# Two-layer graph convolution with a mixture-of-experts block on one core: layer 2 reduces its gathered rows in pairs

## The chip, the cores and the metric

One core of a Trainium2 chip runs the whole program. The metric is the device time of one execution in microseconds; the median of three runs of the kernel before is 1064.74 us.

## The reference

```python
x, src, dst: 1250 nodes of 512 floats, 41250 edges sorted by dst (each node has a loop to itself)

def graph_conv_max(x, src, dst, W_rel, b, W_root):
    agg = segment_max(x[src], dst, num_segments=1250)      # maximum over a node's neighbours
    agg = where(isfinite(agg), agg, 0.0)
    return agg @ W_rel.T + b + x @ W_root.T

h = relu(graph_conv_max(layernorm(x), ..., W1_rel, b1, W1_root))   # layer 1
h = relu(graph_conv_max(h, ..., W2_rel, b2, W2_root))              # layer 2
x = x + h
# then 8 experts, each takes the 512 rows with the highest softmax-over-rows score of its logit:
out_e = gelu(layernorm(x)[idx] @ W1 + b1) @ W2 + b2;  x = x + scatter_add(vals * out_e)
```

## The kernel before, in words

The nodes are sorted by their number of neighbours and cut into ten tiles of 128 (`NQ`), the lightest first. A tile with n neighbours at most needs n rounds: round r fetches for each of the 128 nodes the row of its r-th neighbour (128 rows of 2 KB, out of a table in HBM) and takes the maximum with what is there. Tile 0 has only 98 nodes; its other 30 partitions take over what the heaviest nodes have beyond the limit of the last tile. The last tile passes its maxima through `carry`.

Four parties work on the rounds, and meet only through semaphores:

- GpSimd (POOL) issues one indirect DMA per row of rounds into a ring of 12 slots (`SLOTS`, L884), two to a group (`GROUP`, function `gathers`, L873). Before each group it waits for `done` (the slots are free), for `here` (at most six rows, `FLYING`, under way) and for `s_ic[h]` (the group's two index columns are in `ic`).
- SyncE (SP, function `landed`, L840) waits for each row's landing on `s_gather[j]` and increments `ready` per row (L845), `here` per group (L846), and then loads the group's next two index columns with a DMA of its own (L820, one per group).
- VectorE (DVE) reduces. In layer 1 `pool_pair` (L944) takes two slots in one operation of 128x1024 (L951). In layer 2 `one_round` (L998) takes one slot in an operation of 128x512 (L1004), into the two halves of `acc` in turn; `vec_tile` (L1047) starts a tile with two operations that fill the halves from `carry` (L1057, L1058) and ends it with L1074 to L1080.
- TensorE (PE) and ScalarE (ACT) turn the tile's maxima into the layer's output. In layer 2 PE runs the feed-forward block of tile q (`ffn`, L1178) and in the midst of it the aggregate's product of tile q+1 (`neighbours`, L1146; transposes at L1130, product at L1159), which waits for `fin`, the end of DVE's tile q+1. DVE in turn has done ten rounds of its next tile (`AHEAD`) when it waits for that product (L1026, `add_and_moments`), two more (`PEELED`), and then normalizes (L1044, `normalize`), which lets PE begin the next `ffn`.

In layer 1 PE also makes the first 20 neighbours of every node by one-hot products (L1243), so that layer 1 has 186 gathers and layer 2 338. The counts of rounds are worked out on the device (L664 to L712): layer 1's are rounded up to even for every tile (L665 to L668), layer 2's only in total, by giving the last tile one more round where the sum is odd (L709 to L712).

Of the kernel before, what the change touches and what calls it, by code (L numbers as in the profile page):

```python
# [7 lines left out]
P = 128  # L8
N, E, D = 1250, 41250, 512
# [4 lines left out]
NQ = -(-N // P)  # L14
# [5 lines left out]
SLOTS = 12  # L20
MAXR = 64
UNROLL = 4
FLYING = 6
AHEAD = 10
PEELED = 3 * UNROLL
MINR = PEELED + UNROLL + 1
# [5 lines left out]
GROUP = 2  # L32
SUBS = SLOTS // GROUP
# [43 lines left out]
def build(nc, x, src, dst, w1_rel, b1, w1_root, w2_rel, b2, w2_root, wr, fw1, fb1, fw2, fb2, out):  # L77
    with ExitStack() as ctx:
# [9 lines left out]
        def dram(name, shape, dt=F32):  # L88
# [114 lines left out]
        both1 = sb("both1", [1, NQ], I32)  # L203
        evens, nvalid, base = sb("evens", [NQ, 1], I32), sb("nvalid", [P, NQ]), sb("base", [P, NC])
# [6 lines left out]
        ic = sb("ic", [P, SLOTS], I32)  # L211
# [32 lines left out]
            neg bits bias pairs pa ga merge here""".split()  # L244
        S = {n: sem("s_" + n) for n in names}
        s_gather = [sem(f"s_gather{j}") for j in range(SLOTS)]
        s_ic = [sem(f"s_ic{h}") for h in range(SUBS)]
# [416 lines left out]
        cv.do(v.tensor_scalar(nmax[:, 0:1], nmax[:, 0:1], float(MINR), None, ALU.max))  # L664
        cv.link(v.tensor_scalar(nmax[:, 1:2], nmax[:, 1:2], float(MINP), 1.0, ALU.max, ALU.add))  # L665
        cv.link(v.tensor_copy(evens[:, :], nmax[:, 1:2]))
        cv.link(v.tensor_scalar(evens[:, :], evens[:, :], -2, None, ALU.bitwise_and))
        n_nmax = cv.link(v.tensor_copy(nmax[:, 1:2], evens[:, :]))  # L668
# [38 lines left out]
        cv.do(v.tensor_copy(meta[:, 0:NQ], pl[0:1, 0:NQ]))  # L707
        cv.do(v.tensor_scalar(meta[:, NQ + 1:2 * NQ], pl[0:1, NQ + 1:2 * NQ], -1.0, None, ALU.add))
        cv.link(v.tensor_scalar(meta[:, NQ:NQ + 1], pl[0:1, NQ:NQ + 1], float(GROUP - 1), None, ALU.add))  # L709
        cv.link(v.tensor_scalar(meta[:, NQ:NQ + 1], meta[:, NQ:NQ + 1], -GROUP, None, ALU.bitwise_and))  # L710
        cv.link(v.tensor_tensor(meta[:, 2 * NQ:2 * NQ + 1], meta[:, NQ:NQ + 1], meta[:, NQ - 1:NQ], ALU.subtract))
        n_meta = cv.link(v.tensor_scalar(meta[:, 2 * NQ:2 * NQ + 1], meta[:, 2 * NQ:2 * NQ + 1], -1.0, None, ALU.add))  # L712
# [32 lines left out]
        starts = [a.value_load(meta[0:1, q:q + 1], min_val=0, max_val=(NQ - 1) * MAXR) for q in range(NQ)]  # L745
# [24 lines left out]
        v.sem_inc(S["done"], SLOTS)  # L770
        g.sem_inc(S["here"], FLYING)
        a.wait_ge(S["xs"], 16 * NQ)
        for l in range(2):
# [38 lines left out]
            if l == 0:  # L812
                c = s.value_load(meta1[0:1, NQ:NQ + 1], min_val=NQ * MINP // 2, max_val=NQ * LCAP // 2)
            else:
                c1, c = c, s.value_load(meta[0:1, NQ:NQ + 1], min_val=NQ * MINR, max_val=NQ * MAXR + GROUP) // GROUP
            lists_l = (idx1, idxf)[l]

            def load_indices(i, h):

                s.dma_start(ic[:, h * GROUP:(h + 1) * GROUP], lists_l[:, bass.ds((i * SUBS + h) * GROUP, GROUP)])\  # L820
                    .then_inc(s_ic[h], 16)

            after(s, ca, n_idxf if l else n_idx1s[0])
            for h in range(SUBS):
                if l:
                    s.wait_ge(s_ic[h], ((c1 + (SUBS - 1 - h)) // SUBS + 1) * 16)
                load_indices(0, h)
# [21 lines left out]
            with s.Fori(0, c // SUBS) as i:  # L849
                for h in range(SUBS):  # L850
                    landed(i, h)
            for h in range(SUBS - 1):
                with s.If(c % SUBS > h):
                    landed(c // SUBS, h)
# [767 lines left out]
```

## Time and profile before

| what | value |
|---|---|
| median of 3 runs (lowest, highest) | 1064.74 us (1062.21, 1070.73) |
| profiled execution, span from first to last instruction | 1161.8 us |
| mean granted TensorE clock in it | 0.860 |
| busy: PE, DVE, POOL, ACT | 791.1, 715.0, 627.7, 269.3 us |

For the profiled execution no time of its own is given beside its span, so the span stands for it; it is 97.1 us above the median of the runs, which were made without a profile. Times of rows below are microseconds from the start of the span. A row of a timeline has start, duration, engine, line, operation, and in brackets how long the engine sat idle before it and what released it; "issue" means nothing that the profile shows, "remote" something outside the core's engines. SPq is the sequencer of SP.

### The profile page before, as it was taken

Reading aid. Unit: us, or ns where it says so; the run is one execution under the profiler, and the core shown is the slowest. Engines: PE = TensorE matmul, PEld = TensorE weight load, DVE = VectorE, ACT = ScalarE, POOL = GpSimd, SP = SyncE. Lnnn points to the kernel's source line nnn. Section 1 sums busy time; section 2 is a strip of 40 time slices with the busy share of each in tenths; the row PEclk is TensorE's granted clock in tenths of the full one; section 3 lists DMA queues with packets and bytes.
Section 4 is the critical chain, followed back from the end, with each engine's and each line's share of the span. In section 5 each row is a group of like instructions: output and inputs, shape, how many; then the busy total and the mean of one; then the engine's idle time right before and its main releaser. Section 6 shows DMA issues by size and latency. Waiting matters only on the chain.

```text
span 1161.8 us, 12528 instructions
## 1 busy us (share of the span) xinstructions
PE 791.1 (68%) x2358; PEld 362.5 (31%) x2358; DVE 715.0 (62%) x1428; ACT 269.3 (23%) x436; POOL 627.7 (54%) x627
## 2 busy tenths in 40 slices
PE   0256148888778787550287777869756959777988
PEld 0133013334333333220143333334322424333443
DVE  4769557777666857624565454536543646555888
ACT  0283412333211230010012212122211112212432
POOL 6550363555556656736666645665665476662012
PEclk9778569999998898795688989979887979889989
DMA  5730664666666656586667757765767577776497
GB/s 136 267 104 2 236 184 136 189 189 195 197 189 182 195 175 178 169 288 175 176 175 262 231 164 230 222 209 179 243 211 224 163 233 211 226 213 188 161 380 290
DMA packets 114789, 231.67 MB, mean 199 GB/s; under 512 B 53596, under 2 KB 58080, under 8 KB 111255
## 3 DMA queue, kind: packets, MB, share of 16 engines
q0 software_dynamic: 46304, 149.99, 42.8%
q1 hardware_dynamic: 54346, 38.56, 11.1%
q10 hardware_dynamic: 14092, 42.57, 9.8%
q8 instruction: 19, 0.31, 0.1%
q14 instruction: 28, 0.23, 0.1%
HBM read 196.18 MB, written 37.49 MB: 201 GB/s over the span
## 4 chain that ended last, share of the span: by engine, by line
PE 27%; issue 23%; DVE 22%; another core or an unknown queue 8%; DMA 7%; SPq 5%; ACT 4%; POOL 2%; DVEq 1%; ACTq 1%; POOLq 0%; PEld 0%
PE pp L1194 6%; PE prow L1159 5%; DMA mem<-tab,ic 5%; PE pp L1243 5%; PE pp L1212 5%; DVE mem L1589 2%; DVE acc L940 2%; DVE weights L951 2%; SPq L820 2%; DVE mem L1441 1%; SPq L845 1%; PE pl L1174 1%; POOL mem L884 1%; DVE mem L608 1%
## 5 line engine op out<-in xcount | busy, mean ns | idle before, releaser
L884 POOL DMA_INDIRECT mem<-tab,ic x524 | 546.9, 1044 | 362.3 <-issue 214.8
L1004 DVE TENSOR_TENSOR acc<-acc,mem 128x512 f32<-128x512 f32 x338 | 222.9, 694 | 174.3 <-issue 89.0
L940 DVE TENSOR_TENSOR acc<-acc,pp 128x1024 f32<-128x1024 f32 x90 | 109.7, 1219 | 88.7 <-PE pp L1243 41.5
L1212 PE MATMUL pp<-weights,mem 128*128 128x512 f32 x320 | 152.1, 624 | 14.8 <-issue 12.3
L1194 PE MATMUL pp<-weights,xnT 128*128 128x512 f32 x320 | 152.9, 622 | 0.0
L1243 PE MATMUL pp<-weights,LT 128*128 128x512 bf16 x300 | 81.9, 421 | 62.6 <-DVE acc L940 21.5
L1159 PE MATMUL prow<-weights,aggT 128*128 128x512 f32 x152 | 91.2, 745 | 43.3 <-ACT aggT L1350 33.9
L951 DVE TENSOR_TENSOR weights<-weights,mem 128x1024 f32<-128x1024 f32 x83 | 101.5, 1222 | 9.9 <-DVE weights L951 4.2
L1243 PE MATMUL pp<-weights,slots 128*128 128x512 bf16 x300 | 75.2, 394 | 32.4 <-DVE acc L940 21.7
L1212 PEld LDWEIGHTS pp<-weights,mem 128*128 128x128 f32 x320 | 62.9, 201 | 93.2 <-issue 90.5
L1383 ACT ACTIVATE mem<-pp 128x512 f32<-128x512 f32 x80 | 46.9, 597 | 159.1 <-PE pp L1212 85.1
L1194 PEld LDWEIGHTS pp<-weights,xnT 128*128 128x128 f32 x320 | 59.4, 196 | 70.1 <-issue 70.1
L1243 PEld LDWEIGHTS pp<-weights,LT 128*128 128x128 bf16 x300 | 30.3, 105 | 115.9 <-issue 42.0
L1159 PEld LDWEIGHTS prow<-weights,aggT 128*128 128x128 f32 x152 | 36.2, 245 | 83.7 <-issue 44.2
L1243 PEld LDWEIGHTS pp<-weights,slots 128*128 128x128 bf16 x300 | 29.3, 100 | 79.9 <-DVE acc L940 25.5
L1130 PE MATMUL prow<-ident,agg 128*128 128x128 f32 x80 | 15.2, 322 | 53.9 <-DVE agg L1080 50.4
L1026 DVE TENSOR_TENSOR hst<-prow,mem 128x512 f32<-128x512 f32 x10 | 6.9, 690 | 70.2 <-PE prow L1159 45.4
L1174 PE MATMUL pl<-weights,xnT 128*128 128x512 f32 x80 | 44.1, 681 | 0.0
L1144 PE MATMUL prow<-weights,rootT 128*128 128x512 f32 x80 | 38.6, 605 | 0.0
L1599 POOL DMA_INDIRECT out<-x2t,nodei x1 | 1.3, 1262 | 64.3 <-DVE x2t L1594 64.3
L1375 ACT ACTIVATE mem<-prow 128x512 f32<-128x512 f32 x40 | 23.9, 598 | 46.3 <-remote 36.1
L1575 PE MATMUL pp<-weights,mem 128*128 128x512 f32 x72 | 32.4, 593 | 1.1 <-issue 1.1
(342 smaller groups left out, 888.2 us busy)
## 6 DMA issues: line engine op xcount, KB each, us to landing
yd<-mem ACTq DMA_DIRECT2D x18, 1024.0 KB
weights<-yd SPq DMA_DIRECT2D x9, 2048.0 KB, 13.2
mem<-tab,ic POOLq DMA_INDIRECT x524
weights<-in_L_ffn_W SPq DMA_DIRECT2D x9, 512.0 KB
weights<-in_L_ffn_W ACTq DMA_DIRECT2D x7, 512.0 KB
LT<-ttd ACTq DMA_DIRECT2D x5, 640.0 KB
slots<-ttd ACTq DMA_DIRECT2D x5, 640.0 KB
ic<-idxf SPq DMA_DIRECT2D x175, 1.0 KB
```

The costliest lines, as they stand in the source:

```text
L884: g.indirect_dma_start(rings[l][:, j, :], None, table, bass.IndirectOffsetOnAxis(ic[:, j:j + 1], 0)).then_inc(s_gather[j], 16)
L940: v.tensor_tensor(acc[:, :, :], acc[:, :, :], pp[j % 2][:, :, :], ALU.max).then_inc(S["pa"], 1)
L951: v.tensor_tensor(accg, accg, pair, ALU.max).then_inc(S["done"], 2)
L1004: v.tensor_tensor(acc[:, side, :], acc[:, side, :], rings[l][:, bass.ds(r % SLOTS, 1), :].rearrange("p a d -> p (a d)"), ALU.max).then_inc ...
L1144: t.matmul(pg, rootT[:, c, :], wroot[0][:, c, :], start=False, stop=False)
L1159: ins = t.matmul(pg, aggT[:, c, :], wrel[l][:, c, :], start=l == 1 and c == 0, stop=c == C - 1)
L1174: ins = t.matmul(pl[:, :], xnT[:, c, :], wroot[1][:, c, :], start=False, stop=c == C - 1)
L1194: ins = t.matmul(ph[w % 2].rearrange("p (e f) -> p e f", e=2), xnT[:, c, :], w1s[:, 2 * w:2 * w + 2, c, :], start=False, stop=c == C - 1)
L1212: ins = t.matmul(po[e % 2][:, :], hT[:, e * FC + f, :], w2s[:, e, f, :], start=f == 0, stop=f == FC - 1)
L1243: ins = t.matmul(pp[j % 2][:, k, :], sel[u][:, j * KP + k, :], hot[:, j, w, :], start=w == 0, stop=w == 2)
L1383: a.activation(ystage[:, e, :], po[e % 2][:, :], ACT.Copy).then_inc(S["oe"], 1)
L1575: t.matmul(po[u][:, :], dg[:, u, e, :], expert(q, e), start=e == 0, stop=False)
```

## The change

Layer 2 uses layer 1's pair operation, and both layers count in pairs: each of the 12 pairs of two laps of the ring (`LAP`) has a semaphore that both of its gathers increment, per layer; SP waits once per pair and increments `ready` once; `here` is gone and POOL waits for `ready`. SP loads twelve index columns at a time, after every sixth pair, into one half of an `ic` of 24 columns, and POOL waits for them once per six pairs. Layer 2's count of every tile is rounded up to even. A tile of layer 2 starts with the operation that fills `acc` from `carry` and takes the first pair at once (the first form in `pool_pair`), so that L1057, L1058 and their wait go. The count of rounds before DVE waits for the product stays ten (five pairs), and of those before it normalizes twelve.

```diff
-UNROLL = 4
-FLYING = 6
-AHEAD = 10
-PEELED = 3 * UNROLL
-MINR = PEELED + UNROLL + 1
+FLYING = 3
+AHEAD = 5
+PEELED = 6
+MINR = 2 * (PEELED + 1)
...
+PAIR = 2
+SUBS = SLOTS // PAIR
+LAP = 2 * SUBS
...
-        ic = sb("ic", [P, SLOTS], I32)
+        ic = sb("ic", [P, 2 * SLOTS], I32)
...
-        cv.do(v.tensor_scalar(nmax[:, 0:1], nmax[:, 0:1], float(MINR), None, ALU.max))
+        cv.do(v.tensor_scalar(nmax[:, 0:1], nmax[:, 0:1], float(MINR), 1.0, ALU.max, ALU.add))
...
-        cv.do(v.tensor_copy(meta[:, 0:NQ], pl[0:1, 0:NQ]))
...
+        cv.link(v.tensor_scalar(meta[:, :], pl[0:1, 0:2 * NQ + 1], 0.5, None, ALU.mult))
+        n_meta = cv.link(v.scalar_tensor_tensor(both2[:, :], meta[:, 0:NQ], 64.0, meta[:, NQ + 1:], ALU.mult, ALU.add))
...
-            def landed(i, h):
-
-                before = (c1 + (SUBS - 1 - h)) // SUBS if l else 0
-                for j in range(h * GROUP, (h + 1) * GROUP):
-                    s.wait_ge(s_gather[j], (before + i + 1) * 16)
-                    s.sem_inc(S["ready"], 1)
-                s.sem_inc(S["here"], GROUP)
-                load_indices(i + 1, h)
+            def landed(n, j):
+
+                s.wait_ge(s_gather[l][j], n)
+                s.sem_inc(S["ready"], 1)
+
+            with s.Fori(0, c // LAP) as i:
+                n = s.snap(i * 32 + 32)
+                for j in range(LAP):
+                    landed(n, j)
+                    if j % SUBS == SUBS - 1:
+                        load_indices(i + 1, j // SUBS)
...
+            def gathers(i, j):
+
+                b, h = j // SUBS, j % SUBS
+                g.wait_ge(S["done"], base + i * LAP + (j + 1))
                 g.sem_inc(S["apart_g"], 1)
-                g.wait_ge(S["here"], base + (i * SUBS + h) * GROUP + GROUP)
+                g.wait_ge(S["ready"], base + i * LAP + (j + 1))
...
+                if h == 0:
+                    g.wait_ge(s_ic[l][b], i * 16 + 16)
...
-            def one_round(r, side=0, alternating=True):
...
             def vec_tile(q):
...
-                v.tensor_scalar(acc[:, 0, :], carry[:, :], col, None, ALU.min).then_inc(S["init"], 1)
-                v.tensor_scalar(acc[:, 1, :], carry[:, :], col, None, ALU.min).then_inc(S["init"], 1)
-                v.wait_ge(S["init"], 3 * q + 2)
+                both = v.value_load(both2[0:1, q:q + 1], min_val=MINR // 2, max_val=NQ * MAXR // 2 * 64)
+                lo, m = both // 64, both % 64
+                pool_pair(acc[:, :, :], r1v + lo, lo, cap[:, q:q + 1])
                 if not first:
 
-                    for r in range(AHEAD):
-                        one_round(lo + r, r % 2)
+                    for r in range(1, AHEAD):
+                        pool_pair(acc[:, :, :], r1v + lo + r, lo + r)
                     add_and_moments(q - 1)
...
                     normalize(q - 1)
-                    rounds(lo, m, PEELED)
-                else:
-                    rounds(lo, m)
+                with v.Fori(1 if first else PEELED, m) as i:
+                    pool_pair(acc[:, :, :], r1v + lo + i, lo + i)
```

## Rows read from the trace of the kernel before

**Rows 1.** The page: span; chain that ended last, by engine and by line.

```profile
span 1161.8 us, 12528 instructions
...
PE 27%; issue 23%; DVE 22%; another core or an unknown queue 8%; DMA 7%; SPq 5%; ACT 4%; POOL 2%; DVEq 1%; ACTq 1%; POOLq 0%; PEld 0%
PE pp L1194 6%; PE prow L1159 5%; DMA mem<-tab,ic 5%; PE pp L1243 5%; PE pp L1212 5%; DVE mem L1589 2%; DVE acc L940 2%; DVE weights L951 2%; SPq L820 2%; DVE mem L1441 1%; SPq L845 1%; PE pl L1174 1%; POOL mem L884 1%; DVE mem L608 1%
```

**Rows 2.** Windows by stage; columns as in the first line, us and (x instructions).

```profile
core 0: us, PE busy (x) PEld busy (x) DVE busy (x) ACT busy (x) POOL busy (x), PEclk, DMA share, GB/s
142.00:509.00 367.00, 279.10 (x955) 120.12 (x955) 249.48 (x216) 86.14 (x96) 211.86 (x196) 0.90 0.62 185
509.00:583.00 74.00, 13.76 (x31) 6.03 (x31) 34.31 (x61) 4.69 (x9) 46.57 (x45) 0.62 0.68 196
583.00:964.00 381.00, 289.23 (x756) 133.51 (x756) 199.82 (x369) 73.60 (x137) 236.48 (x233) 0.86 0.69 211
964.00:1076.00 112.00, 85.70 (x217) 38.42 (x216) 64.86 (x128) 23.09 (x43) 63.18 (x63) 0.89 0.69 214
```

**Rows 3.** Timeline of PE in layer 2: start, us, what, [idle before <- releaser].

```profile
723.55 5.62 PE L1159 MATMUL prow<-weights,aggT 128*128 128x512 f32 x8 [6.81 <-ACT aggT L1350]
...
997.83 1.12 PE L1130 MATMUL prow<-ident,agg 128*128 128x128 f32 x4 [4.68 <-DVE agg L1080]
...
1065.90 0.65 PE L1130 MATMUL prow<-ident,agg 128*128 128x128 f32 x4 [1.47 <-DVE agg L1080]
```

**Rows 4.** Windows of L1004 (DVE) per tile: first and last of ten.

```profile
509.00:559.00 50.00, 17.19 (x25) 0.60 0.70 206
...
996.00:1066.00 70.00, 30.33 (x45) 0.83 0.71 214
```

**Rows 5.** Groups by line, window of layer 2: busy us, mean ns | idle before.

```profile
L884 POOL DMA_INDIRECT mem<-tab,ic x338 | 344.6, 1019 | 204.5 <-issue 140.1 <-SPq L846 36.4 <-DVE acc L1004 26.0
L1004 DVE TENSOR_TENSOR acc<-acc,mem 128x512 f32<-128x512 f32 x338 | 222.9, 694 | 174.3 <-issue 89.0 <-remote 45.6 <-SPq L845 23.4
```

**Rows 6.** Windows of L884 (POOL) in layer 1; page group of L951 (DVE).

```profile
142.00:509.00 367.00, 202.28 (x186) 0.90 0.62 185
...
L951 DVE TENSOR_TENSOR weights<-weights,mem 128x1024 f32<-128x1024 f32 x83 | 101.5, 1222 | 9.9 <-DVE weights L951 4.2
```

**Rows 7.** Timelines of POOL and DVE, layer 2, gathers that DVE follows closely.

```profile
539.64 0.95 POOL L884 DMA_INDIRECT mem<-tab,ic  x1 [3.46 <-SPq L846]
...
548.23 1.10 POOL L884 DMA_INDIRECT mem<-tab,ic  x1 [0.30 <-issue]
...
559.83 1.00 POOL L884 DMA_INDIRECT mem<-tab,ic  x1 [0.30 <-issue]
...
547.82 0.69 DVE L1004 TENSOR_TENSOR acc<-acc,mem 128x512 f32<-128x512 f32 x1 [0.72 <-DVE acc L1004]
...
552.25 0.69 DVE L1004 TENSOR_TENSOR acc<-acc,mem 128x512 f32<-128x512 f32 x1 [0.72 <-DVE acc L1004]
```

**Rows 8.** The same two in layer 1, beside pair operations back to back.

```profile
436.76 1.11 POOL L884 DMA_INDIRECT mem<-tab,ic  x1 [0.30 <-issue]
438.18 1.11 POOL L884 DMA_INDIRECT mem<-tab,ic  x1 [0.30 <-issue]
...
437.24 1.23 DVE L951 TENSOR_TENSOR weights<-weights,mem 128x1024 f32<-128x1024 f32 x1 [0.19 <-DVE weights L951]
```

**Rows 9.** The same two in layer 2, DVE catching up row by row.

```profile
914.94 0.95 POOL L884 DMA_INDIRECT mem<-tab,ic  x1 [0.30 <-issue]
916.19 0.95 POOL L884 DMA_INDIRECT mem<-tab,ic  x1 [0.30 <-issue]
...
909.47 8.10 DVE L1004 TENSOR_TENSOR acc<-acc,mem 128x512 f32<-128x512 f32 x13
```

**Rows 10.** Chain of waits in the window 1024:1046, the sequencer of SP.

```profile
1030.88 0.69 SPq L846
1031.57 0.86 SPq L820
```

More of the change, by code:

```diff
@@ L243, in build @@
             ob oe fb2 b2 b2l gd bn rc hs nmx exp apart_s warm apart_g apart_v x2l y out
-            neg bits bias pairs pa ga merge here""".split()
+            neg bits bias pairs pa ga merge""".split()
         S = {n: sem("s_" + n) for n in names}
-        s_gather = [sem(f"s_gather{j}") for j in range(SLOTS)]
-        s_ic = [sem(f"s_ic{h}") for h in range(SUBS)]
+        s_gather = [[sem(f"s_gather{l}_{j}") for j in range(LAP)] for l in range(2)]
+        s_ic = [[sem(f"s_ic{l}_{b}") for b in range(2)] for l in range(2)]
         s_od = [sem(f"s_od{u}") for u in range(2)]
@@ L744, in build @@
         after(a, cv, n_full)
-        starts = [a.value_load(meta[0:1, q:q + 1], min_val=0, max_val=(NQ - 1) * MAXR) for q in range(NQ)]
+        starts = [a.value_load(meta[0:1, q:q + 1], min_val=0, max_val=(NQ - 1) * MAXR // 2) * 2 for q in range(NQ)]
         for q in range(NQ):
@@ L767, in build @@
         t.wait_ge(S["b1"], 16)
-        v.sem_inc(S["done"], SLOTS)
-        g.sem_inc(S["here"], FLYING)
+        v.sem_inc(S["done"], SUBS)
+        g.sem_inc(S["ready"], FLYING)
         a.wait_ge(S["xs"], 16 * NQ)
@@ L814, in build, with load_indices @@
             else:
-                c1, c = c, s.value_load(meta[0:1, NQ:NQ + 1], min_val=NQ * MINR, max_val=NQ * MAXR + GROUP) // GROUP
+                c1, c = c, s.value_load(meta[0:1, NQ:NQ + 1], min_val=NQ * MINR // 2, max_val=NQ * MAXR // 2)
             lists_l = (idx1, idxf)[l]
[L818 to L824, printed above, removed]
+            def load_indices(i, b):
+                s.dma_start(ic[:, b * SLOTS:(b + 1) * SLOTS], lists_l[:, bass.ds((i * 2 + b) * SLOTS, SLOTS)])\
+                    .then_inc(s_ic[l][b], 16)
+            for b in range(2):
+                after(s, ca, n_idxf if l else n_idx1s[b])
                 if l:
-                    s.wait_ge(s_ic[h], ((c1 + (SUBS - 1 - h)) // SUBS + 1) * 16)
-                load_indices(0, h)
+                    s.wait_ge(s_ic[0][b], (c1 // LAP) * 16 + 16)
+                load_indices(0, b)
             if l:
@@ L838, in build @@
                 after(s, ca, n_idx1)
[L840 to L854 removed]
+            def landed(n, j):
[7 more added lines that the diff above has]
+                        load_indices(i + 1, j // SUBS)
+            n = s.snap(c // LAP * 32 + 32)
+            for j in range(LAP - 1):
+                with s.If(c % LAP > j):
+                    landed(n, j)
             with s.Fori(0, 1):
@@ L996, in vec_tile_1 @@
                     cv.link(v.tensor_copy(carry[:, :], agg[:, :]))
-            def one_round(r, side=0, alternating=True):
-                v.wait_ge(S["ready"], r8v + r + 1)
-                v.wait_ge(S["done"], r8v + r + (SLOTS - 1 if alternating else SLOTS))
-                v.tensor_tensor(acc[:, side, :], acc[:, side, :], rings[l][:, bass.ds(r % SLOTS, 1), :].rearrange("p a d -> p (a d)"),
-                                ALU.max).then_inc(S["done"], 1)
-            def rounds(lo, m, first=0):
-                with v.Fori(first // UNROLL, m // UNROLL) as i:
-                    for u in range(UNROLL):
-                        one_round(lo + i * UNROLL + u, u % 2)
-                with v.Fori(0, m % UNROLL + 1) as i:
-                    one_round(lo + m // UNROLL * UNROLL + i, alternating=False)
             def add_and_moments(q):
```

90 lines of the change are left out of this document (36 added, 54 removed).

## Prediction

> **What bounds the kernel now.** I read the chain that ended last, the stages, the engines inside layer 2, and then single gathers beside what DVE does. The chain [rows 1] has no owner: PE 27%, "issue" 23%, DVE 22%. The stages [rows 2] show where the change can act: layer 1 lasts 367 us, layer 2 from 509 to 1076, which is 567 us. In layer 2 PE is 86/112 to 289/381 busy (about 76%), POOL 236/381 (62%), so neither is saturated: they hand each other the lead. PE runs the feed-forward block of a tile, and in most tiles the aggregate is there before PE wants it (at 723.55 PE waits 6.81 us for ACT's copy, not for DVE); at 997.83 PE waits 4.68 us for DVE, at 1065.90 1.47 us [rows 3]. From 509 to 583 PE has nothing to do (13.8 of 74 us busy): DVE must have tile 0 and ten rounds of tile 1, 35 rows, before the first feed-forward block.
>
> So the gathers set the time in the first 74 us and near the end, and a feed-forward period (381 us for the first seven, some 54 each) in between. A tile needs 25 rows at first and 45 at last [rows 4]; the ten counts are 25, 28, 30, 31, 33, 34, 35, 37, 40 and 45.
>
> The span is 1161.8 us, the median 1064.7: the runs are 97 us shorter than what I read. The rows say where that may sit. In layer 2 the sequencers of SP and DVE often need 0.7 us or more for what is otherwise 0.02 to 0.1: SP's increment of `here` took 0.69 and the next register step 0.86 [rows 10], and POOL's and DVE's instructions themselves keep their durations. I take these for the cost of being recorded, mostly. Without them a feed-forward period would be nearer 54 - 97/9 = 43 us (all of the 97 put on nine periods, an estimate), while a gather costs POOL the same: 34 rows at 1.25 to 1.44 us are 43 to 49 us. The unrecorded kernel is then closer to POOL's pace in layer 2 than the profile looks.
>
> **The pace of the gathers.** Undisturbed, a gather is 0.95 us and the next starts 0.30 later: 1.25 us (914.94 to 916.19) [rows 9]. Beside DVE it is longer: the one of 548.23 took 1.10. It ended at 549.33, which is 0.82 after the end of DVE's operation of 547.82 (548.51). In layer 1 the one of 438.18 ended at 439.29, 0.82 after the end of the pair operation of 437.24 (438.47) [rows 7, 8]. So a gather that starts while DVE reads two SBUF operands waits for the end of that operation, and then needs 0.82 more. The mean shows it: 344.6/338 = 1.02 us in layer 2, and 202.28/186 = 1.09 in layer 1, where DVE has 83 pair operations of 1.22 us beside the gathers [rows 5, 6].
>
> The Trainium skill (SBUF — State Buffer, "Who interferes with whom") says that a VectorE instruction with two SBUF inputs and a GpSimd instruction that reads SBUF exclude each other for the whole of the first. By that rule the longer operation blocks longer, and the sum is the one below; if only the number of operations counted, its terms of 0.09 a row would be 0. The trace agrees with the rule, with its 0.82.
>
> **The change, part by part.**
> (a) Even counts. 25, 31, 33, 35 and 37 become 26, 32, 34, 36 and 38; the last tile goes from 45 (which holds the round that made the sum even) to 44. 342 gathers for 338 [rows 4, 5]: at 1.44 us (below) +5.8 us if POOL is the bound everywhere, 0 where the ring was full anyway. Three of the additions (31, 33, and part of 35) lie where PE leads.
> (b) DVE. 338 operations of 0.694 us are 234.6 us; 171 of 1.22 us are 208.6. The 26 us are no gain in time by themselves: DVE was idle 174 us before these very operations [rows 5]. Catching up, 13 single rounds took 8.10 us, 0.62 a row [rows 9]; pairs back to back start every 1.41 us (the gathers beside them run in that step, 436.76 to 438.18), 0.71 a row [rows 8]. No gain there either. L1057 and L1058 go (about 1 us a tile, and a wait); DVE starts a tile with rows waiting in the ring, so I put 0, and -1 to -2 us at the last tile as the low end.
> (c) POOL beside pair operations. Where DVE follows the gathers closely, 14 gathers took 559.83 - 539.64 = 20.2 us, 1.44 each [rows 7]. The geometry gives that: the row gathered at 548.23 is reduced at 552.25, so, less its own delay of 0.15, 3.87 after a start; others give 3.6 to 3.9, I take 3.80. The third gather after it asks for the port 0.13 after its start and waits until 3.80 + 0.69, so three steps are 4.49 - 0.13 and one is 1.45. With a pair operation, 3.80 after the start of the odd gather and 1.22 long, the second pair's first gather would ask at 3.75 + 0.13 and is held to 5.02; solved for a steady step (two pairs less one gather, each pair 2.50 + e: 2e = 3.80 + 1.22 - 0.13 - 3.75) e = 0.57, so 3.07 us a pair, 1.53 a row. That is 0.08 to 0.09 us a row more than now. While DVE catches up the step is 1.41 instead of 1.25, 0.16 more. The bound below is 0, where PE leads or the starts happen to miss each other; the bound above 0.16. I take 0.09.
> (d) SP. Per pair it issues one wait with its increment instead of three such instructions, no increment of `here`, and a sixth of the index DMAs (six waits and one DMA per twelve rows). In the profile this lag is real: in the chain 1030.88 to 1032.44 SP spends 1.55 us on `here` and one register step [rows 10]. If it is only recording, 0 in the runs; if it is there without a profile too, see the first rival. What is late next in the profile is POOL's own 1.25 to 1.44 us a row.
> (e) Index columns twelve at a time. POOL comes back to a half of `ic` twelve gathers later, 15 us at 1.25; SP sends the load once the half's last pair has landed, about 4 us after its issue. Even a load of several us is covered. 0.
> (f) Layer 1: rounds unchanged, DVE unchanged, the SP part of (d). 0. Six small operations at L707 to L712 become two: -0.5 us in the preparation.
>
> **Sum.** Where the gathers lead: the first stretch, 36 rows at 1.53 for 35 at 1.44, is 55.1 - 50.4 = +4.7. From tile 5 on (34, 36, 38, 40 and, after the last product that DVE waits for, 34 rows, 182 for 181 now) 0.09 x 182 + 1.4 = +17.8 if POOL leads throughout. The five steps at 1.44 need 49, 50, 53, 58 and 50 us against periods of about 43, less a ring of 12 rows that POOL may be ahead; so it leads there in the runs, though less surely in the profile's periods of 54. The last pair ends 0.5 us later (1.22 for 0.69), preparation -0.5. All: +22. If PE leads until tile 7, only its 38, 40 and 34 rows count: 0.09 x 112, 10, so +15 with the 4.7. I take +16: on the profile's own time 1161.8 + 16 = 1177.8, less what fewer recorded SP instructions save it (the profile may well show less than before). Durations on POOL and DVE are those of the hardware, so I carry +16 us over to the median: 1064.7 + 16 = 1081. Own range +8 to +30: 1073 to 1095.
>
> **Rivals.**
> *SP's lag was the bound (faster).* For: [rows 10]; the sequencer's slow stretches lie in layer 2. Against: they must be where the 97 us of the profile are. Price: in the first stretch the rows that DVE waits for would be there about 5 us earlier, PE's waits of 4.68 and 1.47 for DVE go [rows 3], and up to 5 us of the rest: -16 us, 1049.
> *PE and ACT lead, and everything else hides (same).* For: PE waits for DVE only twice after 583; POOL has 38% idle. Against: the 97 us. Then only the first stretch counts, +4.7, less 1 to 3 at the end: +3, 1068.
> *The extra waiting is larger (further on the slower side, within my case):* POOL leads from tile 2 on at 0.09 to 0.12 with (a) in full, +35: 1100. It decides from a feed-forward period below about 43 us.
> *The change doesn't do what it says:* if the pairs arrived one by one, DVE would only wait for the second of two; 1.25 us once a tile, hidden but for the last. It changes no case.
>
> **Numbers.** A measurement here can tell about 1% (10.6 us) from no change. Slower case 0.41, same 0.29, faster 0.30. The slower case leans on the 97 us being recording cost and on a steady phase that I derived; the faster one has the most visible waits of the profile behind it. The range takes in both: 1046 to 1098. Chances: faster by over 1% 0.30, within 1% 0.29, slower by over 1% 0.41.
>
> **What would show it.** Right: gathers of L884 in layer 2 with a mean near 1.10 to 1.18 us (now 1.02), each long one ending 0.82 after a pair operation; pairs of gathers about 3.0 us apart where DVE follows; SP with a fraction of its instructions. The first feed-forward block would begin later than 583. Wrong: the mean of L884 stays at 1.02 to 1.05, or PE never waits for DVE between 583 and the end although periods are short, or layer 2 is shorter by more than 15 us in the profile and the runs follow it: then SP and the sequencers were real cost. If both stay equal, PE led all along.

## The result, and the profile after

| kernel | median | lowest, highest | executions |
|---|---|---|---|
| before | 1066.12 us | 1062.21, 1070.73 | 4 |
| changed | 1102.64 us | 1100.61, 1113.29 | 4 |

The ratio is 1.0328, 95% interval 1.0271 to 1.0385: the change costs 3.3%. I had forecast 1081 (1073 to 1095 for the likeliest case, 1046 to 1098 in all): the right sign, less than half the size (16 of 36.5 us), and the result is outside the range.

The profiled execution of the changed kernel took 1102.11 us, 1.81 above its span, and lies within the range of the other three, so recording added nothing that can be seen. That of before, with its span of 1161.8, was of another sort: the runs below fall into two groups, which I call kinds of chips: kind A, on which the kernel before takes 1066 to 1071 us, and kind B, on which it takes 1168 to 1179. No chip was seen in both groups, and one of kind B was measured twice; whether the chip itself makes the difference or something else that ran beside the kernel is not shown. By its span and by its 0.7-us steps on SP the profile of before belongs to kind B, its times to kind A. Where a run below has medians and no ratio, too few of its executions were undisturbed for one.

The page of the changed kernel: span, busy time, and the chain that ended last by engine and by line.

```profile
span 1100.3 us, 10261 instructions
...
PE 781.1 (71%) x2358; PEld 362.7 (33%) x2358; DVE 690.5 (63%) x1237; ACT 270.2 (25%) x436; POOL 677.6 (62%) x631
...
issue 23%; DVE 22%; DMA 21%; PE 16%; POOL 12%; ACT 3%; DVEq 1%; POOLq 1%; ACTq 0%; SPq 0%; PEld 0%
DMA mem<-tab,ic 17%; POOL mem L880 11%; PE pp L1213 6%; PE prow L1129 3%; DVE weights L948 3%; DVE mem L1559 2%; PE pl L1144 2%; DVE acc L937 2%; PE prow L1114 2%; DVE mem L1411 2%; DVE mem L608 1%; DVE acc L986 1%; DVE weights L950 1%; DVE mem L600 1%; DVE acc L939 1%
```

Against [rows 1] DMA went from 7 to 21% and POOL from 2 to 12%: the chain runs through the landings of gathers (17%) and through POOL's line L880. That is not the work of the change: the kernel before with even counts alone, on kind A, has it already:

```profile
DMA 22%; DVE 21%; PE 19%; issue 18%; POOL 13%; ACT 3%; POOLq 3%; DVEq 1%; SPq 0%; ACTq 0%; PEld 0%
```

So on kind A the gathers' pace sets the time of layer 2 before the change too, which the profile of kind B did not show.

Stages of the changed kernel: layer 1, layer 2 up to the first normalized tile, up to the ninth, the last tile. Columns as in [rows 2].

```profile
core 0: us, PE busy (x) PEld busy (x) DVE busy (x) ACT busy (x) POOL busy (x), PEclk, DMA share, GB/s
139.00:497.00 358.00, 279.90 (x974) 122.15 (x974) 249.95 (x216) 87.48 (x99) 217.95 (x196) 0.93 0.65 198
497.00:553.40 56.40, 7.05 (x12) 3.03 (x12) 30.10 (x39) 3.18 (x6) 42.98 (x45) 0.54 0.73 208
553.40:955.00 401.60, 326.52 (x864) 152.61 (x864) 216.53 (x280) 86.77 (x160) 314.88 (x272) 0.89 0.75 234
955.00:1014.20 59.20, 42.85 (x108) 19.93 (x108) 28.67 (x51) 10.90 (x20) 32.19 (x27) 0.82 0.61 190
```

In the middle stage POOL is busy 314.88 of 401.60 us, 78%; [rows 2] had 62%. Since the two profiles are from two kinds of chips, these stages can't be subtracted from those of [rows 2]; the profiles of kind A below serve for that.

Groups by line in layer 2 of the changed kernel (those of [rows 5]):

```profile
L880 POOL DMA_INDIRECT mem<-tab,ic x342 | 390.1, 1140 | 116.4 <-issue 98.6 <-SPq L839 15.1 <-DVE acc L948 2.4
L948 DVE TENSOR_TENSOR acc<-acc,mem 128x1024 f32<-128x1024 f32 x161 | 197.8, 1228 | 211.1 <-SPq L839 203.2 <-DVE acc L948 5.6 <-DVE acc L950 0.7
```

A gather lasts 1.140 us on average, where [rows 5] have 1.019; POOL's idle time before it, 116.4/342 = 0.34 us, is hardly more than the 0.30 between two gathers. In layer 2 POOL hardly pauses: it waits 15.1 us for `ready` and 2.4 for free slots. Waits in layer 2 of the changed kernel:

```profile
engine line waited for: us in total, times, longest us
DVE acc L948 <- SPq L839: 203.2, 116, 4.2
...
PE prow L1100 <- DVE agg L1050: 86.6, 7, 41.6
...
PE prow L1100 <- DVE xin L1023: 39.0, 8, 9.2
```

DVE's pair operations stood still 203.2 us for `ready`, that is for gathers, and PE 86.6 and 39.0 us for DVE (41.6 and 9.2 of it before the first feed-forward block). POOL leads, DVE follows it, PE follows DVE. POOL, then DVE, in tile 3 of the changed kernel (start, duration):

```profile
649.34 1.84 POOL L880 DMA_INDIRECT mem<-tab,ic  x1 [0.30 <-issue]
651.49 0.95 POOL L880 DMA_INDIRECT mem<-tab,ic  x1 [0.31 <-issue]
652.74 1.45 POOL L880 DMA_INDIRECT mem<-tab,ic  x1 [0.30 <-issue]
654.49 0.95 POOL L880 DMA_INDIRECT mem<-tab,ic  x1 [0.30 <-issue]
655.74 1.58 POOL L880 DMA_INDIRECT mem<-tab,ic  x1 [0.30 <-issue]
```

```profile
649.14 1.23 DVE L948 TENSOR_TENSOR acc<-acc,mem 128x1024 f32<-128x1024 f32 x1 [2.17 <-SPq L839]
652.14 1.23 DVE L948 TENSOR_TENSOR acc<-acc,mem 128x1024 f32<-128x1024 f32 x1 [1.77 <-SPq L839]
655.28 1.23 DVE L948 TENSOR_TENSOR acc<-acc,mem 128x1024 f32<-128x1024 f32 x1 [1.92 <-SPq L839]
```

The gather of 649.34 ends at 651.18; the pair operation of 649.14 ended at 650.37, 0.81 earlier. That of 652.74 ends at 654.19 after one that ended at 653.37 (0.82), that of 655.74 at 657.32 after 656.51 (0.81). Here every second gather is held, and a pair takes 3.00 and 3.40 us, where (c) had worked out 3.07.

### The profile page after: what moved, and what is told of

It reads as the page before. It is cut to its first block, busy times and chain, and to the rows that moved or that the text cites. A ratio compares the mean times of both kernels' runs of the same rounds, so it can differ in the third digit from the quotient of the medians.

```text
span 1100.3 us, 10261 instructions
## 1 busy us (share of the span) xinstructions
PE 781.1 (71%) x2358; PEld 362.7 (33%) x2358; DVE 690.5 (63%) x1237; ACT 270.2 (25%) x436; POOL 677.6 (62%) x631
## 4 chain that ended last, share of the span: by engine, by line
issue 23%; DVE 22%; DMA 21%; PE 16%; POOL 12%; ACT 3%; DVEq 1%; POOLq 1%; ACTq 0%; SPq 0%; PEld 0%
DMA mem<-tab,ic 17%; POOL mem L880 11%; PE pp L1213 6%; PE prow L1129 3%; DVE weights L948 3%; DVE mem L1559 2%; PE pl L1144 2%; DVE acc L937 2%; PE prow L1114 2%; DVE mem L1411 2%; DVE mem L608 1%; DVE acc L986 1%; DVE weights L950 1%; DVE mem L600 1%; DVE acc L939 1%
## 5 line engine op out<-in xcount | busy, mean ns | idle before, releaser
L880 POOL DMA_INDIRECT mem<-tab,ic x528 | 595.1, 1127 | 248.6 <-issue 154.7
L948 DVE TENSOR_TENSOR acc<-acc,mem 128x1024 f32<-128x1024 f32 x161 | 197.8, 1228 | 211.1 <-SPq L839 203.2
L1164 PE MATMUL pp<-weights,xnT 128*128 128x512 f32 x320 | 158.2, 640 | 0.0
L1182 PE MATMUL pp<-weights,mem 128*128 128x512 f32 x320 | 142.4, 592 | 0.0
L1213 PE MATMUL pp<-weights,LT 128*128 128x512 bf16 x300 | 78.0, 406 | 48.1 <-DVE acc L939 16.6
L1129 PE MATMUL prow<-weights,aggT 128*128 128x512 f32 x152 | 85.3, 703 | 8.7 <-ACT aggT L1320 8.0
L1182 PEld LDWEIGHTS pp<-weights,mem 128*128 128x128 f32 x320 | 59.9, 190 | 70.8 <-issue 70.8
L1100 PE MATMUL prow<-ident,agg 128*128 128x128 f32 x80 | 14.3, 307 | 88.3 <-DVE agg L1050 86.6
L1129 PEld LDWEIGHTS prow<-weights,aggT 128*128 128x128 f32 x152 | 33.5, 227 | 45.8 <-issue 31.6
L1100 PE MATMUL prow<-ident,xin 128*128 128x128 f32 x80 | 15.4, 323 | 44.8 <-DVE xin L1023 41.0
L1100 PEld LDWEIGHTS prow<-ident,agg 128*128 128x128 f32 x80 | 10.4, 156 | 93.2 <-DVE agg L1050 47.0
L1545 PE MATMUL pp<-weights,mem 128*128 128x512 f32 x72 | 32.4, 593 | 1.4 <-issue 1.4
```

Of the source, the lines that this page charges most:

```text
L880: g.indirect_dma_start(rings[l][:, h * PAIR + k, :], None, table, bass.IndirectOffsetOnAxis(ic[:, j * PAIR + k:j * PAIR + k + 1], 0))\
L948: v.tensor_tensor(into, into, pair, ALU.max).then_inc(S["done"], 1)
L1100: ins = t.transpose(dst_bank[:, c * P:c * P + P], in_[:, c * P:c * P + P], ident[:, :])
L1129: ins = t.matmul(pg, aggT[:, c, :], wrel[l][:, c, :], start=l == 1 and c == 0, stop=c == C - 1)
L1164: ins = t.matmul(ph[w % 2].rearrange("p (e f) -> p e f", e=2), xnT[:, c, :], w1s[:, 2 * w:2 * w + 2, c, :], start=False, stop=c == C - 1)
L1182: ins = t.matmul(po[e % 2][:, :], hT[:, e * FC + f, :], w2s[:, e, f, :], start=f == 0, stop=f == FC - 1)
```

## The experiments

The edits are shown shortened: only the lines that matter, without the calls around them, and with names such as `row_k` for a longer expression.

### Undoing one part at a time (chip of kind A)

**Even counts alone** in the kernel before:

```diff
-evens = sb("evens", [NQ, 1], I32)
+evens = sb("evens", [NQ, 2], I32)
-v.tensor_scalar(nmax[:, 0:1], nmax[:, 0:1], float(MINR), None, ALU.max)
+v.tensor_scalar(nmax[:, 0:1], nmax[:, 0:1], float(MINR + 1), 1.0, ALU.max, ALU.add)
-v.tensor_copy(nmax[:, 1:2], evens[:, :])
+v.tensor_copy(nmax[:, :], evens[:, :])
```

> The kernel before with nothing but the even counts of layer 2 (342 gathers for 338). If the gathers set layer 2's pace, four more cost 4 x 1.4 us: 1070-1074 us. If even counts were the cost of the change, 1090 us or more; if PE leads, 1064-1068 us.

Measured: 1076.57 us against 1071.22, ratio 1.0042 (1.0004 to 1.0081). The four rows cost 4.5 us (0.0042 x 1071; the interval allows 0.4 to 8.7), near the top of (a)'s 0 to 5.8. It is also the base for the rest, with the changed kernel's 342 rows on kind A. Its groups in layer 2:

```profile
L884 POOL DMA_INDIRECT mem<-tab,ic x342 | 357.5, 1045 | 126.1 <-issue 110.4 <-SPq L846 9.2 <-DVE acc L1004 6.6
L1004 DVE TENSOR_TENSOR acc<-acc,mem 128x512 f32<-128x512 f32 x342 | 227.8, 693 | 167.6 <-SPq L845 156.7 <-DVE acc L1004 5.7 <-DVE acc L1058 3.0
```

The gathers are busy 357.5 us here, 390.1 in the changed kernel: 32.6 us more. The gathers' own windows, up to the first normalized tile and from there to the last gather, for this kernel and then for the changed one:

```profile
495.30:556.80 61.50, 48.09 (x45) 0.57 0.71 191
556.80:970.20 413.40, 308.50 (x298) 0.91 0.81 248
```

```profile
497.00:553.40 56.40, 42.98 (x45) 0.54 0.73 208
553.40:994.20 440.80, 345.97 (x298) 0.89 0.75 234
```

After the first tile a row costs 413.4/298 = 1.387 us here and 440.8/298 = 1.479 in the changed kernel: 0.09 a row, as predicted, but on all 298 rows. The first stretch went the other way: 61.5 and 56.4. The profiled execution of even counts, 1081.09 us, was 4.5 us above its kernel's median, so these differences are better taken from the next kernel, whose profiled execution (1076.56) lies at its median.

**The changed kernel with shorter operations in layer 2**: pairs, semaphores, SP and index loads as changed, only the operation is cut, in two (shown) and in four of 256 columns.

```diff
+if l:
+    for k in range(2):
+        ins = v.tensor_tensor(flat[:, k * 512:k * 512 + 512], flat[:, k * 512:k * 512 + 512], row_k, ALU.max)
+    ins.then_inc(S["done"], 1)
+    return
```

> The changed kernel whole, except that in layer 2 each pair is reduced by two operations of 128x512 instead of one of 128x1024. If the length of DVE's operation is what delays the gathers, the mean of a gather in layer 2 falls from 1.14 to 1.02-1.06 us and the time from 1103 to 1066-1076 us (what is left over the kernel before is the four added rows). If it is the waiting for both rows of a pair, the shared semaphore, or the index loads by twelve, the time stays at 1095 us or more and the mean of a gather stays near 1.14.

> The same with four operations of 128x256 for a pair. If a gather waits for the end of the one operation that runs when it asks, shorter ones hold it less: mean of a gather 0.98-1.03 us, time 1055-1072 us. If a gather has to wait until DVE pauses, four operations in a row hold it at least as long as one of 1024: time 1100 us or more.

Measured: two operations 1076.57 us, ratio 1.0038 (1.0007 to 1.0069), the same as even counts alone. Four: 1065.82 us, 0.9947 (0.9911 to 0.9983), although DVE's time in them rises: half a per cent below the kernel before, with four rows more. Groups in layer 2, of the kernel with two operations and of that with four:

```profile
L880 POOL DMA_INDIRECT mem<-tab,ic x342 | 360.9, 1055 | 119.3 <-issue 96.1 <-SPq L839 22.1 <-DVE acc L955 1.1
L955 DVE TENSOR_TENSOR acc<-acc,mem 128x512 f32<-128x512 f32 x322 | 208.5, 689 | 169.9 <-SPq L839 157.9 <-DVE acc L955 8.3 <-DVE acc L957 1.9
```

```profile
L880 POOL DMA_INDIRECT mem<-tab,ic x342 | 344.6, 1008 | 122.4 <-issue 83.6 <-SPq L839 32.1 <-DVE acc L955 5.5
L955 DVE TENSOR_TENSOR acc<-acc,mem 128x256 f32<-128x256 f32 x644 | 231.1, 421 | 130.0 <-SPq L839 115.3 <-DVE acc L955 11.5 <-DVE acc L957 1.4
```

The same two windows of the gathers as above, for the kernel with two operations:

```profile
493.80:551.90 58.10, 44.96 (x44) 0.57 0.71 200
551.90:965.10 413.20, 315.05 (x299) 0.92 0.80 249
```

So the loss beyond the four rows is the length of the operation: 1140 ns a gather with 1.23 us operations, 1055 with 0.69, 1008 with 0.42, and from the first to the last gather 497.2 us (56.4 + 440.8) with the long operation against 471.3. Semaphore per pair, SP's shorter work and the loads of twelve columns together bring or cost nothing here that the intervals would show, which leave about 5 us either way. For gathers begun while such an operation ran I took the duration above the undisturbed 0.946 us from the timeline: a mean of about 0.4 us in the changed kernel, 0.2 with two operations, 0.1 with four (some 150 to 190 gathers each).

**The pair reduced by an operation with one operand** (`two` is the pair, its two rows side by side for each element; the slots come free after it, and a 128x512 maximum follows):

```diff
+    v.tensor_reduce(acc[:, 1, :], two, AX.X, ALU.max).then_inc(S["done"], 1)
+    v.wait_ge(S["done"], r + (SUBS + 1))
+    v.tensor_tensor(acc[:, 0, :], acc[:, 0, :], acc[:, 1, :], ALU.max).then_inc(S["red"], 1)
...
-v.tensor_tensor(acc[:, 0, :], acc[:, 0, :], acc[:, 1, :], ALU.max).then_inc(S["init"], 1)
```

> The changed kernel, but in layer 2 each pair is first reduced to one row by a tensor_reduce (one SBUF operand), and that row goes into acc by an operation of 128x512 with two SBUF operands. DVE works longer on a pair (1.1 + 0.7 us for 1.22). If only operations with two SBUF operands hold the gathers up, no gather waits for the reduce, the mean of a gather is 1.00-1.04 us and the time 1050-1072 us. If any busy time of DVE did it, the mean would rise above 1.14 and the time to 1110 us or more.

Measured: 1063.62 us, ratio 0.9882 (0.9819 to 0.9945): 1.2% below the kernel before, with four rows more, and over 4% below the changed one. Groups in layer 2, then POOL and DVE early in tile 5:

```profile
L881 POOL DMA_INDIRECT mem<-tab,ic x342 | 338.1, 989 | 123.8 <-issue 79.5 <-SPq L840 31.1 <-DVE acc L954 13.3
L954 DVE TENSOR_REDUCE acc<-mem 128x512 f32 x171 | 211.0, 1234 | 70.5 <-SPq L840 38.0 <-DVE acc L957 21.0 <-issue 8.5
...
L957 DVE TENSOR_TENSOR acc<-acc 128x512 f32<-128x512 f32 x161 | 112.4, 698 | 5.6
```

```profile
710.01 0.95 POOL L881 DMA_INDIRECT mem<-tab,ic  x1 [0.30 <-issue]
711.27 0.95 POOL L881 DMA_INDIRECT mem<-tab,ic  x1 [0.30 <-issue]
```

```profile
709.09 1.23 DVE L954 TENSOR_REDUCE acc<-mem 128x512 f32 x1 [0.20 <-DVE acc L957]
...
711.25 1.24 DVE L954 TENSOR_REDUCE acc<-mem 128x512 f32 x1 [0.20 <-DVE acc L957]
```

The gather of 710.01 begins beside the reduction of 709.09, and that of 711.27 just after the reduction of 711.25 has begun; both take 0.95 us. Some 160 gathers began beside these reductions, and they waited under 0.01 us on average. DVE is busy 211.0 + 112.4 us where it had 197.8, and the kernel is faster. The Trainium skill (SBUF — State Buffer, "Who interferes with whom") says that `tensor_reduce` on trn2 never contends with GpSimd, and that a VectorE instruction with at most one SBUF input, outside its two-port modes, does not; this trace agrees, under 0.01 us against about 0.4.

### Undoing the index loads (chip of kind A)

**Two columns per load again**, in both layers, loaded after every pair, all else as changed; beside it the changed kernel unedited.

```diff
-s.dma_start(ic[:, b * SLOTS:(b + 1) * SLOTS], lists_l[:, bass.ds((i * 2 + b) * SLOTS, SLOTS)])
+s.dma_start(ic[:, j * PAIR:(j + 1) * PAIR], lists_l[:, bass.ds((i * LAP + j) * PAIR, PAIR)])
-g.wait_ge(s_ic[l][b], i * 16 + 16)
+g.wait_ge(s_ic[l][b], i * (16 * SUBS) + 16 * SUBS)
```

> The changed kernel with its index columns loaded two at a time again, one DMA of SP per pair in both layers (some 33,000 packets of 8 bytes more), everything else as in the changed kernel. Where the kernel before takes about 1070 us: my (e), that these loads cost nothing, gives the changed kernel's time within 0.5%. Where it takes about 1165 to 1180 us (PE and ACT stand idle there for no cause that the profile shows): if the change's gain there comes from the 33,000 packets fewer, the gain goes, ratio 0.99 to 1.01 against the kernel before, and PE's idle time under `issue` in layer 2 rises from 38 to 54 us to about 70 to 90; if not, it equals the changed kernel of the same job within 1%.

> The changed kernel beside the run above, unedited. Where the kernel before takes about 1070 us: 1.03. Where it takes about 1165 to 1180 us: 0.96 to 0.985. If it is 0.99 or more there, the change gains nothing on that kind of chip, and the 0.963 of the run with more SP instructions was chance.

Measured: 1104.05 us, ratio 1.0323 (1.0279 to 1.0366), and the unedited change 1102.23 us, 1.0322 (1.0278 to 1.0365). The packets, with loads per pair and in the changed kernel:

```profile
DMA packets 115393, 232.68 MB, mean 209 GB/s; under 512 B 53948, under 2 KB 58432, under 8 KB 111863
```

```profile
DMA packets 82273, 232.66 MB, mean 211 GB/s; under 512 B 20828, under 2 KB 25312, under 8 KB 78743
```

33,120 packets more cost nothing that can be measured: (e) holds on kind A, and the loss of the change came out again, 3.2% here. The unedited change's gathers, in the same two windows as above:

```profile
492.90:556.60 63.70, 50.26 (x45) 0.54 0.65 184
556.60:992.70 436.10, 337.79 (x298) 0.90 0.76 237
```

Here the first stretch took 63.7 us where the first profile had 56.4, for the same kernel and nearly the same total. Over tile 0 (rows 0 to 25) the mean step was 1.51 in one and 1.275 in the other. The other profiles with the long operation fall near the same two levels: 1.49 with loads per pair, and on kind B, below, 1.27 and 1.50 in the two profiles of the unedited change and 1.46 with more increments by SP. So in a stretch where nothing else disturbs POOL and DVE, the starts of gathers and operations seem to miss each other all the time or to meet all the time; what decides between the two is not shown.

### Chips of kind B

**The kernel before, and its rounds cut in two**, on a chip of kind B; the cut was run on two of them.

```diff
-v.tensor_tensor(acc[:, side, :], acc[:, side, :], row, ALU.max).then_inc(S["done"], 1)
+for d in (0, D // 2):
+    ins = v.tensor_tensor(acc[:, side, d:d + D // 2], acc[:, side, d:d + D // 2], row_d, ALU.max)
+ins.then_inc(S["done"], 1)
```

> The kernel before, unchanged, for a second profile of it. If the 97 us between its first profile and its runs were the cost of that one recording, the span now is 1062 to 1078 us, the long steps of SP's and DVE's sequencers are gone, and POOL hardly pauses in layer 2 (338 gathers in 465 to 475 us). If they belong to this kernel whenever it is recorded, the span is again above 1140.

> The kernel before with each round of layer 2 done by two operations of 128x256 instead of one of 128x512; 338 gathers, all else unchanged. If the length of the operation alone delays the gathers, the mean of a gather falls from 1.05 to 1.00-1.02 and the time by 5 to 15 us, 0.5 to 1.4%. If DVE's extra work per round counts (two starts for one), it rises by as much.

> The kernel of the sixth run again. On a chip of about 1070 us: 0.5 to 1.4% faster than before by the shorter operations; on one of about 1178 us the same ratio as measured there, 1.00 to 1.01.

Measured: before 1178.83 us (19 executions); the cut 1182.78, ratio 1.0063 (1.0006 to 1.012), and on the second chip 1177.4 against 1167.64, 1.0193 (1.0068 to 1.0318). The profiled execution of before took 1183.95 us, 0.4% above the median of the others on that chip. So 97 us of recording do not exist; the first profile of before showed what such a chip does. The shorter gathers (1.011 us for 1.023) bring nothing there; both ratios lie above 1.

**The one-operand reduction with its second operation cut in two, and also with layer 1's pair operation cut in two**, on two chips of kind B.

```diff
+for d in (0, D // 2):
+    ins = v.tensor_tensor(acc[:, 0, d:d + D // 2], acc[:, 0, d:d + D // 2], acc[:, 1, d:d + D // 2], ALU.max)
...
+for k in range(2):
+    ins = v.tensor_tensor(into[:, k, :], into[:, k, :], row_k, ALU.max)
```

> The kernel of the fourth run (pair reduced by a one-operand tensor_reduce), with the accumulation into acc in two operations of 128x256 instead of one of 128x512. By the port, the mean of a gather falls from 0.989 to 0.96-0.98 and the time by 3 to 8 us. If DVE has become the bound by then, the time stays or rises by up to 5 us.

> The kernel of the seventh run again. On a chip of about 1070 us: the mean of a gather 0.96-0.98 and 1052-1062 us, 1 to 2% faster than before; on one of about 1178 us the ratio measured there, 0.99 to 1.01.

> The kernel of the fourth run, with the pair operations of layer 1 also cut into two of 128x512. The gathers of layer 1 get shorter (from 1.10 to about 1.04 us), but if POOL doesn't lead there, nothing is gained, and DVE, which PE waits for, has 83 x 0.1 to 0.2 us more to do: 0 to +15 us against the fourth run. If the port mattered wherever gathers run, it would be 5 us or more faster.

> The kernel of the eighth run again. On a chip of about 1070 us, if POOL doesn't lead in layer 1: 1062-1078 us, no better than the fourth run's 1063.6; if it does, below 1058.

Measured, first kernel: 1180.24 us, 1.0025 (0.994 to 1.011), and 1159.75, 1.0002 (0.9945 to 1.0058). Second: 1163.1, 0.9861 (0.9746 to 0.9976), and 1164.22, 1.0054 (1.0001 to 1.0106). The two chips contradict each other on the second kernel, and none of the four shows a gain that repeats. A mean gather of 0.96 to 0.98 us instead of 1.02 is worth next to nothing on this kind.

**The changed kernel there**, twice:

> The changed kernel, unaltered, beside the kernel before on one chip. If the chip is one on which the kernel before takes about 1067-1072 us, this takes 1100-1106, as measured. If it is one on which it takes about 1178 us (the sequencers of SP and DVE make 0.7 us steps, and the feed-forward periods last 50 to 60 us), POOL does not lead; then the longer gathers hide mostly and fewer SP instructions may help: 1165-1190 us, within 1.5% of before. If the loss is there at full size (over 2.5%), the gathers lead on that chip too.

> The changed kernel once more, unedited, on whatever chip this is. Theory: the sign of the change depends on the kind of chip. Where the kernel before takes about 1065 to 1075 us, POOL leads all of layer 2 and the change loses: ratio 1.03. Where the kernel before takes about 1160 to 1180 us (0.7-us steps on the sequencers of SP and DVE in its profile), SP's lag leads and the change gains: ratio 0.97 to 0.985, with a layer-2 pace of about 1.57 us a row. Rival: the 2.3% gain seen on the slow kind was one chip's drift between executions; then the ratio lies within 1% of 1.

Measured: 1141.09 us (1118.0 to 1149.33) against 1167.64, and 1160.61 us (1123.61 to 1166.84) against 1176.55, without a ratio: the medians are 2.3% and 1.4% below. The changed kernel spreads there by 3 to 4% from execution to execution, so the size is uncertain, but each of its executions (1149.33 and 1166.84 at most) was faster than every one of before beside it (1152.63 and 1173.37 at least): the 3.3% loss is absent, and the change gains. Waits in layer 2 of before (the first profile), then of the changed kernel on such a chip, and one stall from the latter's timeline of PE:

```profile
DVE acc L1004 <- issue: 89.0, 89, 12.3
...
DVE acc L1004 <- remote: 45.6, 24, 4.6
...
PE prow L1130 <- issue: 36.9, 7, 14.6
...
ACT mem L1375 <- remote: 36.1, 12, 5.9
```

```profile
DVE acc L948 <- issue: 105.7, 61, 5.8
...
PE prow L1100 <- issue: 43.3, 5, 20.0
ACT weights L1341 <- remote: 37.5, 6, 13.6
```

```profile
865.08 1.09 PE L1100 MATMUL prow<-ident,rootT 128*128 128x128 f32 x4 [19.98 <-issue]
```

PE stood 36.9 and 43.3 us at one line for `issue`, that is with no releaser that the profile shows, once for 19.98 us; DVE and ACT likewise, and for `remote`. On kind A neither the changed kernel nor that with even counts has one such wait of PE's matmuls or of ACT in layer 2, and DVE's waits without a shown releaser sum to 10 to 15 us, where they are 175 here in before (129.7 issue, 45.6 remote, over all its lines) and 134 in the second profile of the changed kernel there.

**Who brings the gain there?** More increments by SP after each pair in layer 2, the two-operation kernel, and the one-operand kernel:

```diff
 s.wait_ge(s_gather[l][j], n)
 s.sem_inc(S["ready"], 1)
+for _ in range(4 * l):
+    s.sem_inc(S["apart_s"], 1)
```

> The changed kernel with four more increments by SP after each pair's `ready` in layer 2, so that SP again issues about as many instructions per pair as before the change. Theory (SP costs nothing where its steps are short): equal to the changed kernel within 0.5% on a chip where the kernel before takes about 1070 us. On one where it takes about 1165 us and SP's steps last up to 0.7 us: SP's lag comes back, 10 to 30 us more than the changed kernel, which is ratio 0.99 to 1.01 against the kernel before. Rival (the gain there comes from elsewhere: fewer DVE instructions, or fewer DMAs for index columns): equal to the changed kernel there too.

> The changed kernel with each layer-2 pair reduced by two operations of 128x512. Where the kernel before takes about 1070 us: 1.004 as before. Where it takes about 1165 us: if the change's gain there comes from SP and the longer operation still costs its share, this gains more than the change, 0.96 to 0.975; if DVE's own sequencer is slow there too (each further instruction costs up to 0.7 us), the second operation costs about what it saves and this equals the changed kernel within 0.5%.

> The changed kernel with the one-operand reduction of each pair in layer 2, for a second interval. Where the kernel before takes about 1070 us: 0.988 as the first time. Where it takes about 1165 us: if SP's steps alone are slow, it gains both what the change gains and the blocking, 0.965 to 0.975; if DVE's steps are slow too (it has one more wait and instruction per pair), near the changed kernel or above it, 0.98 to 1.0.

Measured against 1176.55 us: SP's increments 1145.69 us, ratio 0.9633 (0.9569 to 0.9698, from its two lowest executions); two operations 1168.76 us, 0.9896 (0.9818 to 0.9974); one operand 1171.7 us, no ratio. The chain of waits of the kernel with more increments, and its waits in layer 2:

```profile
941.39 0.70 SPq L841
942.11 0.70 SPq L841
```

```profile
DVE acc L950 <- SPq L839: 123.7, 63, 4.6
...
PE prow L1102 <- issue: 17.6, 5, 9.8
```

SP's steps of 0.7 us are back and even in the chain, and the time from the end of a pair's last gather to its `ready` rose from a mean of 3.17 to 3.79 us. No slowing is shown: the median is below the changed kernel's 1160.61, the lowest execution above it (1133.07 for 1123.61). But the edit gives back only part of SP's lag: in the two profiles of the kernel before on this kind the same time has a mean of 4.8 us, on kind A (even counts alone) 3.4. More is told by the kernels above that have the change's SP part and its loads of twelve columns, and more than one operation of DVE per pair. In their profiles on kind B the time to `ready` is 3.1 us too, and they take 0.986 to 1.005 of before. So neither the shorter lag, the mechanism of my first rival, nor the fewer index loads alone brings the 1141 to 1161 us.

Nor do the unexplained stalls go with the time from kernel to kernel: those of PE's matmuls in layer 2 sum to 69 and 82 us in the two profiles of before and to 38 to 54 in the three with the long operation, but to 24 in a profiled execution of 1181.03 us (one operand, second operation cut) and to 90 in one of 1144.55 (one operand). What the three measurements of 1141 to 1161 us share is one operation of DVE per pair, the fewest instructions on DVE. Whether that is the cause stays open.

## Why the prediction was wrong where it was

**(a) Even counts**, 0 to 5.8: measured 4.5 us (0.4 to 8.7). Right, toward its upper end; that three of the additions lie "where PE leads" is not borne out, since POOL hardly stopped.

**(c) POOL beside pair operations.** The mechanism is right: 0.82 after the end of DVE's operation, 3.00 and 3.40 us a pair in the rows shown, mean gather 1.140 (forecast 1.10 to 1.18). The size per row is right as a difference: 0.09 to 0.10 us more in the first profile of the change, 0.08 in the second, against even counts or two operations. Both levels lie below those worked out (1.38 to 1.39 and 1.46 to 1.48 us a row, for 1.44 and 1.53), so that the difference fits so well is in part luck.

**The step that failed** is "From tile 5 on ... 0.09 x 182": from which tile POOL leads. It was held against "periods of about 43, less a ring of 12 rows". With even counts alone the first two periods between normalized tiles are 42.4 and 39.7 us, and PE does not wait for DVE in them; from the third on (42.7, then 46 to 56 us) it waits for DVE's `xin` or aggregate in every one. So 40 to 42, and not 43, is what PE needs, and 30 to 32 rows at 1.39 us already take 42 to 45. By my own numbers tiles 3 and 4 (31 and 33 rows at 1.44, 45 and 48 us against 43) would have been led by POOL; the credit for the ring put that off to tile 5. But a ring is a head start and no rest: POOL waited for slots and for `here` only 15.8 us in all of layer 2 with even counts and 17.5 in the changed kernel, so nearly every lengthening of a gather moved the end, on 298 rows and not 182. That is 0.09 x 298 = 27 us where I had 16. Then I took +16 from a sum of +22, on account of a case in which PE leads until tile 7, which moved the forecast further from what came.

**The sum against the record.** From the first to the last gather the changed kernel takes 25.9 us more than the one with two operations in the first profile (497.2 for 471.3) and 28.5 in the second (499.8). With the four rows' 4.5 that makes 30 to 33, of the 36.5 measured (1102.64 - 1066.12). The remainder of 4 to 6 is not assigned. The last pair's 0.5 was not measured by itself.

**First stretch, +4.7.** Against two operations (58.1) the two profiles give -1.7 and +5.6, against even counts (61.5) -5.1 and +2.2. The steady phase that I derived (1.53 a row) is real in one (1.51) and absent in the other (1.275). It is not a term with one value.

**The 97 us.** "I take these for the cost of being recorded, mostly" was wrong: the profile comes from a kind of chip on which sequencers lag and PE and ACT stand still. What I needed from it, that the timed runs have shorter periods than the profile, was true all the same, so the sign came out in part by luck: had the times come from the profile's kind of chip, the change would have gained. [rows 1] already held the hint: "issue 23%; another core or an unknown queue 8%"; the waits of PE by cause would have shown 36.9 us of `issue` at L1130, 69.1 over all of PE's matmuls, and these are no waits for SP. I also wrote that "PE waits for DVE only twice after 583"; the timeline has a third such wait, for `xin`, nearly as long as the longer of the two:

```profile
1020.21 0.66 PE L1130 MATMUL prow<-ident,xin 128*128 128x128 f32 x4 [4.54 <-DVE xin L1044]
```

**The rivals.** "The extra waiting is larger", 1100 us with POOL leading from tile 2 and periods under 43, is what happened, with its deciding point. I ended the range at 1098 and so below it. "SP's lag" did not decide on kind A, where `ready` came 3.4 us after a gather before and 3.2 after the change; on kind B, where the change does gain, kernels with the lag gone do not show the gain. "PE and ACT lead" was wrong on kind A; on kind B the length of the gathers mattered as little as it says, but the time fell instead of staying. The pairs do arrive as the change says.

**(b), (d), (e), (f)** at 0: together consistent with two operations giving 1.0038 beside 1.0042 for even counts alone, and (e) by the loads per pair, 1.0323 beside 1.0322. (b) by itself was not separated: its fewer microseconds of DVE belong to the longer operation. (f)'s -0.5 is below what a run can tell.

## What to carry to other kernels

Where GpSimd's indirect DMAs set the pace, the length of a VectorE operation with two SBUF operands is a price on the gather, so two short operations can beat one long one that has less busy time, and an operation with one operand is free for the gathers even when DVE's total rises. Before a gap between a profile's span and the runs' median is taken for the cost of recording, list the waits by cause: if engines stand still for `issue` and `remote`, the profile may come from another chip than the times, and each stage's bound must then be taken anew. And if a rival is the forecast's own mechanism with one condition shifted (from which tile POOL leads), the range must reach past its number.

## What was not expected of the hardware

- The same program takes 1066 to 1071 us on some chips (three sets of measurements, two of them on known chips, 7 and 5) and 1168 to 1179 on others (three sets, chips 3, 0 and 3 again). On the latter, single sequencer steps of SP and DVE last 0.70 us, and PE and ACT have stalls of up to 20 us without a shown cause.
- A gather that begins beside a two-operand operation ends 0.82 us after that operation's end where it is held, with 128x1024, 128x512 and 128x256 alike; of several operations back to back it waits for the end of the one that runs. Beside `tensor_reduce`, or an operation with one operand in SBUF and one in PSUM (L940, layer 1), the delay is under 0.01 us.
- The same kernel's first stretch of layer 2, up to the first normalized tile, took 56.4 us in one profile and 63.7 in another, with steps of 1.275 and 1.51 us between gathers.
